# First block turned and split tile by tile, its seeds copied from a spread row, block 1's root on ScalarE, tanh of two blocks kept in SBUF

## The reference

```python
xn = (x - mean(x)) / sqrt(var(x) + 1e-5)                  # over the 256 features
h = tanh(xn @ W1.T + b1);  s = h @ w2.T + b2              # one score per token
e = exp(s - max over the sequence)
ctx = cumsum(e * xn) / cumsum(e)                          # along the sequence
attn = tanh(concat(ctx, xn) @ Wc.T + bc)
gate, up = xn @ (w_gate / 127).T, xn @ (w_up / 127).T
ffn = (silu(gate) * up) @ (w_down / 127).T
out = x + attn + ffn
```

## Time and profile before

| | |
|---|---|
| median of 3 runs | 393.62 us (392.67 to 393.69) |
| the profiled execution's own time | 393.06 us |
| its span (first to last instruction) | 391.1 us |
| TensorE busy | 385.9 us, 99% |
| VectorE, ScalarE, GpSimd busy | 76%, 60%, 54% |
| first score sum, first gate sum, last product begins to be read | 9.12, 11.74, 387.78 us |

### The profile page before, as it was taken

One profiled execution on the slowest core, in us unless ns is written; L12 is line 12 of the kernel. 1 busy time (PEld: TensorE's weight loads), 2 busy tenths in 40 slices (PEclk: granted clock), 3 DMA queues, 4 the chain that ended last, 5 costly groups with the idle time before them and its releaser, 6 DMA issues.

```text
span 391.1 us, 7885 instructions
## 1 busy us (share of the span) xinstructions
PE 385.9 (99%) x2740; PEld 268.7 (69%) x2740; DVE 297.5 (76%) x632; ACT 235.6 (60%) x434; POOL 210.1 (54%) x289
## 2 busy tenths in 40 slices
PE   8999999999999999999999999999999999999996
PEld 4556676757566686866877676767677676676765
DVE  6799998999996997876769966777676765754351
ACT  4766576689985659786556575364553644536250
POOL 1487586874629989794335405866456554502000
PEclk9999999999999999999999999999999999999999
DMA  8944525576834232475210005043231220100001
GB/s 275 348 158 69 137 53 134 106 189 89 201 72 96 54 83 81 116 165 97 76 34 29 27 28 164 28 128 87 58 72 55 90 85 26 54 28 28 28 28 61
DMA packets 54945, 36.56 MB, mean 93 GB/s; under 512 B 31858, under 2 KB 50292, under 8 KB 54900
## 3 DMA queue, kind: packets, MB, share of 16 engines
q1 hardware_dynamic: 54608, 35.73, 35.5%
q10 hardware_dynamic: 292, 0.26, 0.2%
HBM read 20.19 MB, written 8.45 MB: 73 GB/s over the span
## 4 chain that ended last, share of the span: by engine, by line
PE 97%; DVE 2%; issue 0%; DVEq 0%
PE bank L707 44%; PE bank L743 41%; PE bank L763 9%; PE bank L1381 1%; DVE ex L1121 0%; DVE stats L951 0%; PE bank L700 0%; PE bank L1377 0%; DVE veps L980 0%; DVE xt L1091 0%; DVE bank L1116 0%; DVE sg L1413 0%; PE bank L813 0%; DVE mv L955 0%; PE bank L819 0%
## 5 line engine op out<-in xcount | busy, mean ns | idle before, releaser
L743 PE MATMUL bank<-xt,narrow 128*128 128x512 f16 x768 | 177.3, 379 | 0.0
L743 PEld LDWEIGHTS bank<-xt,narrow 128*128 128x128 f16 x768 | 75.2, 98 | 75.4 <-DVE wide L1121 0.2
L707 PE MATMUL bank<-narrow,wide 128*128 128x256 f16 x792 | 96.4, 273 | 0.0
L707 PE MATMUL bank<-narrow,xt 128*128 128x256 f16 x768 | 92.8, 273 | 0.3 <-DVE xt L1091 0.3
L707 PEld LDWEIGHTS bank<-narrow,xt 128*128 128x128 f16 x768 | 75.0, 98 | 19.0 <-DVE xt L1091 0.6
L1258 POOL TENSOR_TENSOR wide<-ex,wide 128x512 f16<-128x512 f32 x32 | 39.4, 1248 | 87.6 <-ACT wide L909 87.6
L888 ACT ACTIVATE sg<-bank 128x512 f32<-128x512 f32 x96 | 57.2, 596 | 46.3 <-PE bank L743 45.6
L1116 DVE SCALAR_TENSOR_TENSOR bank<-bank,sg 128x512 f32<-128x512 f32 x96 | 66.1, 694 | 24.4 <-PE bank L743 21.3
L707 PEld LDWEIGHTS bank<-narrow,wide 128*128 128x128 f16 x792 | 77.5, 98 | 9.4
L895 ACT ACTIVATE wide<-bank 128x512 f16<-128x512 f32 x90 | 53.3, 596 | 47.7 <-DVE bank L1116 39.3
L1121 DVE TENSOR_TENSOR wide<-bank,wide 128x512 f16<-128x512 f32 x90 | 60.5, 678 | 9.9 <-ACT wide L895 8.6
(11 more groups left out here) (103 smaller groups left out, 262.3 us busy)
## 6 DMA issues: line engine op xcount, KB each, us to landing
rows<-scratch SPq DMA_DIRECT2D x16, 512.0 KB, 5.1
out_y<-xres SPq DMA_DIRECT2D x31, 256.0 KB, 2.1
xres<-in_x SPq DMA_DIRECT2D x15, 512.0 KB, 5.1
xt<-xt SPq DMA_TRANSPOSE x56, 2.5
wide<-in_wg SPq DMA_DIRECT2D x1, 768.0 KB, 5.9
wide<-in_wu SPq DMA_DIRECT2D x1, 768.0 KB, 8.4
wide<-in_wd SPq DMA_DIRECT2D x1, 768.0 KB, 10.1
wide<-in_wc SPq DMA_DIRECT2D x1, 512.0 KB, 11.1
```

Of the source, the lines that this page charges most:

```text
L707: return pe.matmul(dst, lhs, rhs, start=False, stop=stop, skip_group_check=True)
L743: mm = pe.matmul(b[:, :], pg.up(which, k, j), pg.xn(sx, k, tok), start=n == 0, stop=n == len(todo) - 1)
```

## The change

Block 0 no longer goes through `Lb`, `Xh`, `Xl`. Each of its four tiles is normalised with a signal of its own, turned by two transposes (`L0`), read out (`X0`, ScalarE, 128x256) and its rest taken (`Y0`, VectorE). Its score sums are one TensorE list: high x high for all four tiles, as each `X0` comes, then high x rest for all four, then rest x high as each `Y0` comes. The step `Ea` is gone: TensorE spreads only `b1`, and the two seeds of block 0 are read by ScalarE straight from bank 7; `b1` and `w2` come into SBUF for the later blocks by two further broadcast loads on SyncE's list. The square roots of blocks 0 and 1 are both `Sqrt` with epsilon as the activation's bias; block 1's (`Rq`) must come before `Tb`, and `Tb` before the first tanh; GpSimd has no Newton steps for block 1. The tanh of blocks 0 and 1 is written into `rows` in SBUF, so its bank is free after `Th`, and `Sv` of these blocks is due 25 us after its sum. `Wgh` and `Wuh` are cut into halves. The warm-up is 9 products and 4 fills before the turns, none behind them. The planner's assumptions are changed with it.

```diff
+AWAY = 2
+ROOTS = 2
-    "Ea": (SE, 0.5, 0.63), "Tb": (SE, 1.4, 1.5), ...
+    "Tb": (SE, 1.4, 1.5), "Rq": (SE, 0.25, 0.35), ...
-    "Wgh": (PO, 1.5, 1.6), "Wuh": (PO, 1.5, 1.6), ...
+    "Wgh": (PO, 0.77, 0.87), "Wuh": (PO, 0.77, 0.87), "L0": (TE, 0.22, 0.35), "X0": (SE, 0.31, 0.43), "Y0": (VE, 0.36, 0.49), ...
+WARM, FILL = 9, 4
+ROW_BANK = BANKS - 1
-BEGIN = {TE: 7.3, SE: 5.7, VE: 8.1, PO: 1.0, SY: 12.0}
+BEGIN = {TE: 6.9, SE: 5.6, VE: 7.8, PO: 1.0, SY: 12.0}
-X_SENT = (0.0, 11.1, 20.0)
+X_SENT = (0.0, 10.4, 20.0)
-        turn = 2.5 + 3.55 * (i - 1) if i else -2
+        turn = (2.0 if i == 1 else 2.5 + 3.55 * (i - 1)) if i else -2
-            due["Ss", i, pr] = due["S", i, pr] - (1.6 if i or not pr else 0.6)
-            due["Th", i, pr], due["Sv", i, pr] = end["S", i, pr] + 0.1, end["S", i, pr] + 0.8
+            due["Ss", i, pr] = due["S", i, pr] - 1.6 if i else -3.5 + 0.1 * pr
+            due["Th", i, pr], due["Sv", i, pr] = end["S", i, pr] + 0.1, end["S", i, pr] + (25.0 if i < AWAY else 0.8)
...
     if kind == "Tb":
-        return [(("Xh", 0, 1), 0)]
+        return [(("X0", 0, 3), 0), *((("Rq", g, 0), 0) for g in range(1, ROOTS))]
+    if kind == "Rq":
+        return [(("B", i, 1), 0)]
...
     if kind == "Th":
-        return [(("S", i, x), 0)]
+        return [(("S", i, x), 0), *([] if i or wide else [(("Tb", 0, 0), 0)])]
...
+                if kind == "S" and i < AWAY:
+                    return a_s, self.nth("Th", i, n)
...
+        def turn_tile(pe, t):
+            pe.wait_ge(v_xn, t + 1)
+            for k in range(KD):
+                mm = pe.transpose(bank_of(fits, "L0", 0, t)[:, k * P:(k + 1) * P], xnat[:, t // 2, t % 2, k * P:(k + 1) * P], ident[:, :])
+            mm.then_inc(p_x0, 1)
+
+        def first_scores(pe, pr):
+            def onto(t, sx, sw, stop=False):
+                for k in range(KD):
+                    mm = pe.matmul(bank_of(fits, "S", 0, t // 2)[:, t % 2 * D:(t % 2 + 1) * D], fits.xn(sx, k, slice(t * P, (t + 1) * P)),
+                                   fits.w1(sw, k), start=False, stop=stop and k == KD - 1, skip_group_check=True)
+                return mm
+            if not pr:
+                pe.wait_ge(a_w, 1)
+                for t in range(4):
+                    pe.wait_ge(a_ss, t // 2 + 1)
+                    pe.wait_ge(a_x0, t + 1)
+                    onto(t, 0, 0)
+                pe.wait_ge(v_w, 1)
+                for t in range(4):
+                    onto(t, 0, 1)
+            for t in (2 * pr, 2 * pr + 1):
+                pe.wait_ge(v_x0, t + 1)
+                mm = onto(t, 1, 0, True)
+            mm.then_inc(p_s, 1)
...
+        def square_root(act, g):
+            act.wait_ge(v_mv, 2 * g + 2)
+            act.activation(rstd[:, columns(g)], mv[:, columns(g), 1], ACT.Sqrt, bias=eps[:, 0:1]).then_inc(a_root, 1)
...
             elif kind == "Ss":
-                act.wait_ge(a_b, 1)
                 act.wait_ge(p_warm, 1)
-                bias_seed(act, pg, 0, open_bank(act, pg, "S", i, n), a_ss)
+                if i or pg.wide:
+                    act.wait_ge(s_b1, 16)
+                    bias_seed(act, pg, 0, open_bank(act, pg, "S", i, n), a_ss)
+                else:
+                    act.wait_ge(p_b, 1)
+                    spread_row(act, pg, bank[ROW_BANK][:, 0:D], open_bank(act, pg, "S", i, n), a_ss)
...
-            step(dve.tensor_scalar(veps[:, t], mv[:, t, 1], EPS, None, ALU.add))
-            dve.tensor_scalar(minus_half[:, t], veps[:, t], -0.5, None, ALU.mult)
-            dve.wait_ge(a_root, 1)
+            dve.tensor_scalar(minus_half[:, t], mv[:, t, 1], EPS, -0.5, ALU.add, ALU.mult)
+            dve.wait_ge(a_root, g + 1)
...
-                    h = bank_of(pg, "S", i, n)[:, t * D:(t + 1) * D]
+                    h = (rows[:, i, n, :] if i < AWAY else bank_of(pg, "S", i, n))[:, t * D:(t + 1) * D]
...
             sp.dma_start(half(wu32.bitcast(I32)), rows_of(wu)).then_inc(s_wu, 16)
+            sp.dma_start(b1_every, biases[0:D].partition_broadcast(P)).then_inc(s_b1, 16)
             sp.dma_start(wd32.bitcast(I32).rearrange("p (k n) -> p k n", k=KH), rows_of(wd)).then_inc(s_wd, 16)
             load_x(sp, 2)
+            sp.dma_start(w2b, w2b2_in[0:D].partition_broadcast(P)).then_inc(s_w2, 16)
...
-            for n in range(FILL):
-                warm_up(spare_bank)
+            for n in range(FILL):
+                warm_up(FITS.place["L0", 0, 0])
             pe.wait_ge(s_ident, 16)
             for kind, i, n in FITS.early(TE):
                 tensor_step(pe, fits, kind, i, n)
-                if (kind, i, n) == ("Lb", 0, 1):
-                    for n in range(FILL):
-                        warm_up(spare_bank)
```

More of the change, by code:

```diff
@@ L316, in needs @@
     if kind == "C":
[L317 removed]
+        return [(("Cs", i, x), 0), (turned(min(x, 1)), 0), *((("Cl", i, k), 1.3 + 0.65 * k) for k in range(KD)),
                 (("C", i, x - 1) if x else ("Wcl", 0, 0), 0)]
@@ L442, in start @@
         _, busy, seen = STEP[st[0]]
+        if st[:2] == ("S", 0) and not self.wide:
+            busy, seen = (0.44, 0.68) if st[2] else (2.18, 2.42)
         if st[0] in ("C", "D") and len(tiles_of(*st[1:])) == 1:
```

231 lines of the change are left out of this document (132 added, 99 removed).

## The result

The changed kernel is slower by 1%: 397.11 us median of 5 runs (396.17 to 397.79) against 393.62 of before (392.67 to 393.97, 5 runs); ratio 1.0095, 95% interval 1.0079 to 1.0111. The forecast was 392.9 us, "same", with a range that ended at 394.3. The profiled execution took 397.79 us for a span of 396.0 (before: 393.06 for 391.1).

A forecast was written before the change was run, and what follows sets the result against it. TensorE, busy 99% of the span, was taken as the bound, so time follows the first gate sum and the one hole: -0.35 - 0.33 = -0.68 us, giving 392.9 us from the median of 393.62; range 391.9 to 394.3.

The forecast's parts named there:

- part 3 (b): VectorE: 3.1 us of `Sv` move to about 35 to 55 us; cost 0, at worst 3.1 us.
- (c): SyncE's queue: two broadcast loads of 128 KB behind `wu` make nothing used before later; cost 0.
- the sign: VectorE: the forecast would be wrong if moved `Sv` stands before what a TensorE wait after 35 us needs.
- R4: Rival: `Tb` behind block 1's root starves TensorE of banks; 1 us beyond gives 393.9 us; chance 0.05 with another new wait.
- another new wait: Rival: some new wait not further named, sharing a chance of 0.05 with R4.
- R3: Rival: TensorE's clock falls at the leaner start, 1.9 us lost, 394.8 us; chance 0.08.
- Part 1, the start: Start of the kernel: gate sums begin at 11.39 instead of 11.74, gain 0.35 us; bounds 0.47 gain to 0.07 loss.
- three waits: TensorE's first score pass: waits of about 0.09 us, three times, for the next X0.
- Part 2, the hole: Block 1's scores: TensorE's wait for `Xl` at 24.21 goes away, gain 0.33 us; bounds 0 to 0.33.
- Part 3 (a): ScalarE: table load moves from 10.02 to 12.4, behind block 1's root; TensorE's free banks cover it; cost 0.
- (d): Halves of `Wgh` and `Wuh`: an up sum can start on half; cost 0.

The follow-up runs named there:

- The runs above: The kernel before with only the change's warm-up (9 products, 4 fills before the turns, none behind): 393.36 us, ratio 1.0013; four of 12 runs at 395.04 to 396.16.
- the early load: Changed kernel with the load of `w2` moved right behind that of `b1`, ahead of `wd`: 393.56 us, ratio 0.9991.
- the held kernel: Changed kernel with `Sv` of blocks 0 and 1 not taken before 24.0 of the plan: 393.27, 393.74 and 392.39 us; ratios 0.9990, 1.0011, 0.9994.
- the two held versions: Changed kernel with `Sv` held and the old warm-up: 392.95 us, ratio 0.9984; with block 3's root seed held too: 392.71 us, ratio 0.9982.
- the later load: Changed kernel with the load of `w2` moved behind those of `wc` and `tri`: 397.55 us, ratio 1.0096.
- `AWAY = 0`: Changed kernel with the tanh of blocks 0 and 1 left in PSUM and `Sv` due at once: 396.05 us, ratio 1.0071.

## Why the prediction was wrong, step by step

**The step that failed** is part 3 (b) with (c). (b) read the due time of `Sv` as its place: "The 3.1 us of Sv go to about 35 to 55 us". But a due time is a priority only. The planner takes, when an engine is idle, the ready step that is due first, and VectorE was idle when the tanh came at 14.7 of the plan, so `Sv` (due at 27.2) went there, ahead of the first H (due at 5.4, but not ready). In place of the cost of 0 the runs showed a wait of TensorE of 2.80 us, 2.96 by starts, and 1.69 us of low clock behind it. (c) said of the new loads that "nothing used before is later"; it asked who used the queue before, not who on VectorE would now wait for the new row. The planner's table knows no landing for `w2`, so nothing kept `Sv` back until 17.47. The prediction even named the sign, "if the moved Sv stands before what a TensorE wait after 35 us needs", but looked for it 15 us too late. The earlier trace rows gave 6.6 us for such a row; the new one was issued at 8.72, behind 768 KB of `wd` and 512 KB of x, and took 8.75. Moved ahead of both it was issued at 4.69 and took 9.8, so it is the place on the list, and not the time in flight, that made it late.

**What the wait cost.** None of the rivals had this mechanism; R4's "or another new wait" at 0.05 names none. R4 (TensorE without a free bank between 14 and 20) had the victim right and the cause wrong: `Tb` didn't hold it up (table load 13.22, first tanh 14.62, forecast 13.9); what TensorE waited for, from 19.31, was ScalarE's seed, and that stood on ScalarE's list behind the `Hh` of the late H. R3 had the price of a low clock right (half of the stretch) and its place wrong: the start of this execution was early, and the clock fell behind the new wait. The last product came 5.09 us later than the sum had it (+4.41 against -0.68): the wait and the clock, 2.96 + 1.69, are most of it, the wait for `sg` is 0.76, and the start and the hole gave 0.22 more than forecast. The Trainium skill (page "TensorE: Matmul & The Clock Gate", section "Part 1: The HAM clock gate") calls the lower clock the default and says that the moment of the rise differs from run to run; the trace agrees, with scores of one and the same kernel before at 9.12 and at 9.91.

**Part 1, the start.** The first X0 at 7.88 (8.02 forecast), the scores from 8.65 (8.49), the second gate sum 0.40 us earlier than before (0.35 forecast). The term was right in this trace, in part by luck: all eight turns stand ahead of the scores on TensorE's list, which cost the 0.16, and the first pass was hardly paced (20 products in 2.25 us, 0.113 each), which gave back most of the 0.27 that the sum had put there for three waits. Its assumption was not right: that nine products always reach the higher clock because twelve did in one trace. That trace was of an early rise. The runs above price the assumption at 0 in the median and 2 to 3 us in four of twelve executions, and it is one of the reasons that the profiles show for the kernels without the wait not having the 0.68 us in full; the others are the wait for `sg` with the early load, and the wait of the down sum with `Sv` held.

**Part 2, the hole.** Gone, as forecast, and it returns (0.54 us) when the root does. The prediction took its size from the listed idle time, 0.33 us; by starts it was 0.50. The normalisation of block 1 began at 15.28, not 13.65: its statistics waited for x until 10.91 (forecast 10.05), and two small operations took 0.83 and 0.68 us beside GpSimd's conversion instead of 0.2. Nothing waited for it.

```profile
12.91 0.83 DVE L1104 TENSOR_SCALAR minus_half<-mv 128x4 f32<-128x4 f32 x1
...
13.84 0.68 DVE L1107 TENSOR_TENSOR newton<-rstd 128x4 f32<-128x4 f32 x1
...
12.88 1.63 POOL L1347 TENSOR_SCALAR narrow<-wide 128x768 f16<-128x768 int32 x2 [1.72 <-DMA wide<-in_wu]
```

**Part 3 (a) and (d).** Cost 0, as forecast, in what TensorE saw.

**What no part had.** Every VectorE step was priced by its own row; that some rows hold only while GpSimd is quiet wasn't asked, though the change moves GpSimd's large steps by some us (block 1's normalisation from 19.51 to 15.28) and puts an input of `Sv` into SBUF. It was 1.27 us of the first delay. At the first down sum it came again, but in kernels of the experiments and not in the changed one.

## What to carry to other kernels

When a step is given a later due time, read the list that the planner writes: an idle engine takes it early, and if one of its inputs is a load that the planner doesn't know, everything behind it waits. Price a wait on TensorE with the clock that falls behind it: here a wait of 2.96 us brought 1.69 us more. When one of GpSimd's large steps moves, look which small VectorE operations come to lie beside it; and when a step is held back, look what the planner puts in its place.

## What the runs showed of the hardware

Some VectorE operations wait for GpSimd's step to end, though they are small themselves. `Sv` with both inputs in SBUF took 1.68 us beside a conversion and 0.42 without it; with its first input in PSUM it took 0.43 beside the same conversion. Operations on 128x4 take 0.16 us, and took 0.83, 1.15 and 1.22 beside GpSimd; these end within some 0.05 us of the end of one of its operations. It goes the other way as well: in the kernel with the early load, four normalisations of GpSimd took 3.13 us beside `Sv` instead of 2.17.

```profile
15.36 3.13 POOL L1334 TENSOR_SCALAR xnat<-xres,rstd,shift 128x256 f32<-128x256 f32 x4 [0.78 <-DVE shift L1112]
```

The Trainium skill (page "SBUF — State Buffer", section "SBUF: two separate sides") describes the port pair that the two engines share as an exclusive lock, held for a whole instruction, which a VectorE operation takes in a two-port mode, or with two SBUF inputs against a GpSimd operation that reads SBUF. The trace agrees for `Sv`, by the numbers above; that the operations on 128x4, most with one input, run in such a mode is not shown.

TensorE's clock rises at different moments in different executions of one program. Twelve warm-up products took 4.18 to 5.30 us; the first score product of the kernel before came at 9.12 and at 9.91, that of the held kernel at 10.00, 8.32 and 8.41. Of eleven profiles of the changed kernel and its versions with nine products, six have it at 8.14 to 8.65 and five at 10.00 to 10.04. With twelve products ahead of the row, the runs of the two held versions spread over 0.8 and 1.1 us, those of the kernel before (23 to 35 on a chip) over 1.3 to 1.7; with nine, over 1.2 to 3.4, and over 4.0 in the four runs with the later load. What decides the moment stays open; no run here tells.

A clock once reached can fall within the kernel, and it fell after the work had resumed: behind a wait listed with 2.80 us, the granted clock was 0.84 and 0.73 of full speed in the stretches of 4 us around and behind it, with the fall near 22.7 and products again from 22.11. Behind the 2.98 us of the later load it was 0.92 and 0.65. After the 1.54 us wait at 33.7 in the held kernel, and the 1.45 us with `AWAY = 0`, it stayed at 1.00.
